# A hybrid transformer on one core: where values, projections and weighings stand in their steps, and embedded values in strips of 32 columns

## The reference

```python
att = jnp.einsum('bhtd,bhsd->bhts', q, k) * scale + jnp.einsum('bhtd,tsd->bhts', q, rk)
att = jax.nn.softmax(jnp.where(causal[None, None], att, -jnp.inf), axis=-1)
y = jnp.einsum('bhts,bhsd->bhtd', att, v) + jnp.einsum('bhts,tsd->bhtd', att, rv)
```

## Time and profile before

| | us |
|---|---|
| median of three runs | 3053.79 |
| the profiled execution | 3039.37 |
| its span, first to last instruction | 3037.6 |
| TensorE busy | 2790.9 |
| VectorE busy | 1947.6 |
| ScalarE busy | 1885.4 |
| GpSimd busy | 1055.3 |

### The profile page before, as it was taken

The page is one execution under the profiler, slowest core; times in us unless marked ns, Lnnn a source line. Parts: engine busy times, 40 slices in busy tenths (PEclk is TensorE's granted clock), DMA queues, the critical chain, the costliest instruction groups (busy, mean ns, idle before and its releaser), DMA issues.

```text
span 3037.6 us, 58842 instructions
## 1 busy us (share of the span) xinstructions
PE 2790.9 (92%) x21780; PEld 1904.2 (63%) x21780; DVE 1947.6 (64%) x5625; ACT 1885.4 (62%) x4404; POOL 1055.3 (35%) x876
## 2 busy tenths in 40 slices
PE   8889989978999999789999999898899998998997
PEld 5565647537888886378888888455355464554554
DVE  6454636376777775778888887675476324764774
ACT  6666766514666764167777777586587514875774
POOL 2222223203233230064545453354255112552551
PEclk9999999988999998999999999999999999999999
DMA  1010000000000000200000000310111001110210
GB/s 52 3 38 1 12 9 1 4 8 1 2 2 2 2 2 3 72 2 2 2 2 2 2 2 2 123 47 21 40 49 32 22 1 54 49 32 24 51 39 14
DMA packets 35262, 62.83 MB, mean 21 GB/s; under 512 B 11526, under 2 KB 15654, under 8 KB 33830
## 3 DMA queue, kind: packets, MB, share of 16 engines
q1 hardware_dynamic: 34982, 59.07, 7.0%
HBM read 23.48 MB, written 1.15 MB: 8 GB/s over the span
## 4 chain that ended last, share of the span: by engine, by line
PE 72%; DVE 10%; ACT 7%; issue 4%; POOL 3%; SPq 2%; DMA 1%; DVEq 0%; POOLq 0%; ACTq 0%
PE bank L779 62%; PE bank L1004 6%; PE bank L1119 3%; SPq L745 2%; POOL work L1903 2%; ACT bank L1245 1%; ACT work L1237 1%; ACT squared L1247 1%; DVE work L1610 1%; ACT work L1269 1%; DVE centered L1481 1%; DVE normed L1488 1%; ACT work L1361 1%; ACT squared L1241 1%; DVE work L1754 1%
## 5 line engine op out<-in xcount | busy, mean ns | idle before, releaser
L1325 ACT ACTIVATE low<-bank,low 128x512 f32<-128x512 f32 (+23 forms) x384 | 227.4, 593 | 331.0 <-DVE low L1667 326.9
L1237 ACT ACTIVATE low<-bank 128x512 f32<-128x512 f32 (+3 forms) x512 | 425.6, 941 | 0.9 <-PE bank L1004 0.9
L779 PE MATMUL bank<-table_keys,halves 128*128 128x512 f32 (+3 forms) x1536 | 419.1, 381 | 0.6 <-ACT low L1325 0.4
L779 PE MATMUL bank<-work 128*64 128x128 f32 (+6 forms) x4480 | 368.2, 291 | 41.0 <-DVE work L1557 16.1
L1667 DVE TENSOR_REDUCE low<-bank 128x1 f32<-128x512 f32 (+22 forms) x512 | 289.5, 572 | 166.1 <-PE bank L779 161.8
L779 PEld LDWEIGHTS bank<-work 128*64 128x64 f32 (+3 forms) x4480 | 266.8, 145 | 192.3 <-issue 143.5
L1857 POOL TENSOR_TENSOR halves<-squared,const 128x512 fp32r<-128x512 f32 x128 | 135.4, 1058 | 578.4 <-PE bank L779 578.4
L1237 ACT ACTIVATE work<-bank 128x512 f32<-128x512 f32 (+4 forms) x389 | 200.8, 539 | 165.1 <-PE bank L779 63.4
L779 PEld LDWEIGHTS bank<-table_keys,halves 128*128 128x128 f32 x1536 | 245.7, 192 | 55.9 <-issue 33.7
L1903 POOL TENSOR_TENSOR work<-work 128x768 f32<-128x768 f32 x128 | 187.7, 1466 | 193.6 <-DVE work L1758 190.5
L1361 ACT ACTIVATE work<-work 128x192 f32<-128x192 f32 (+1 forms) x512 | 218.8, 431 | 49.1 <-DVE work L1747 49.1
(11 more groups left out here) (198 smaller groups left out, 5900.9 us busy)
## 6 DMA issues: line engine op xcount, KB each, us to landing
work<-work SPq DMA_DIRECT2D x512, 64.0 KB, 2.0
slot<-in_wW SPq DMA_DIRECT2D x4, 1605.5 KB, 6.7
slot<-in_wA SPq DMA_DIRECT2D x4, 837.0 KB, 6.1
table_low<-embv_padded SPq DMA_DIRECT2D x2, 1536.0 KB, 6.3
table<-in_dft SPq DMA_DIRECT2D x1, 3072.0 KB, 11.8
slot<-in_wE SPq DMA_DIRECT2D x2, 584.0 KB, 3.9
const<-in_const SPq DMA_DIRECT2D x1, 1094.5 KB, 5.0
squared<-in_x SPq DMA_DIRECT2D x4, 256.0 KB, 6.1
```

Of the source, the lines that this page charges most:

```text
L779: return pe.matmul(o, l, r, start=start, stop=stop)
L1237: return act.activation(dst, src, ACT.Identity)
L1325: act.activation(PR[t.G % 4][:, 0:n], bank[t.G % 2][:, 0:n], ACT.Exp, bias=NBR[:, t.G % 4:t.G % 4 + 1], accum_out=RSR[:, t.G % 8:t.G % 8 + ...
```

## The change

Four things.

1. In A the values of window i-2 stand behind the context, the projections, the output projection and the norm, before the weighing. Since the next lane's context is now made before a lane's last values, `CN` and `QT` have two buffers.
2. In A the feed-forward is split in `a_mlp` (up and Gelu) and `a_mlp_down` (down and residual). Between the two of lane 3 stand the next layer's projection of lane 0 and its linear part, which no longer stand in step 0 (but in the first layer).
3. In W the inversion and weighing of j stand in step j, behind scores, exponentials and scaling, instead of at the head of step j+1. POOL's shift waits for the weighings ahead of it.
4. In R each embedded matmul of 64 columns is issued as two of 32.

```diff
@@ LAST_READ
-    "a_mlp": each("a_gelu", 4) + STREAM,
+    "a_mlp": each("a_gelu", 4),
+    "a_mlp_down": STREAM,
@@ make_plan, stage_a, the loop
-                if i == 0:
+                if i == 0 and layer == 0:
                     add("a_project", c=0)
                 if i < C * NT:
                     add("a_scores", c=c, w=w, i=i)
-                if i == 0:
+                if i == 0 and layer == 0:
                     add("a_linear", c=0)
                 if w == 3 and c + 1 < C:
                     add("a_linear", c=c + 1)
-                if 2 <= i <= C * NT + 1:
-                    if (i - 2) % NT == 0:
-                        held = add("a_values", c=(i - 2) // NT, w=0, i=i - 2)
-                    else:
-                        add("a_values_on", c=(i - 2) // NT, w=(i - 2) % NT, i=i - 2, tile=held)
-                    if (i - 2) % NT == NT - 1:
-                        add("a_heads", c=(i - 2) // NT, tile=held)
                 if w == 1 and c < C:
                     add("a_context", c=c)
...
                 if w == 0 and 2 <= c:
                     add("norm_scale", c=c - 2, **second)
+                if 2 <= i <= C * NT + 1:
+                    if (i - 2) % NT == 0:
+                        held = add("a_values", c=(i - 2) // NT, w=0, i=i - 2)
+                    else:
+                        add("a_values_on", c=(i - 2) // NT, w=(i - 2) % NT, i=i - 2, tile=held)
+                    if (i - 2) % NT == NT - 1:
+                        add("a_heads", c=(i - 2) // NT, tile=held)
                 if i < C * NT:
                     add("a_weigh", c=c, w=w, i=i)
@@ behind the loop
+            def mlp(c):
+                up = add("a_mlp", c=c, load=load)
+                add("a_mlp_down", c=c, load=load, tile=up)
...
                 add("norm_mean", c=0, **first)
-                add("a_mlp", c=2, load=load)
+                mlp(2)
                 add("norm_scale", c=0, **first)
                 add("norm_mean", c=1, **first)
-                add("a_mlp", c=3, load=load)
+                up = add("a_mlp", c=3, load=load)
+                add("a_project", c=0)
+                add("a_linear", c=0)
+                add("a_mlp_down", c=3, load=load, tile=up)
                 add("norm_scale", c=1, **first)
                 add("norm_mean", c=2, **first)
@@ stage_w
-                if 1 <= j <= len(pairs):
-                    lane, i, hp = pairs[j - 1]
-                    add("w_weigh", c=lane, i=i, hp=hp)
...
                 if lane_items <= r - 2 < C * lane_items:
                     scale(r - 2)
+                if j < len(pairs):
+                    lane, i, hp = pairs[j]
+                    add("w_weigh", c=lane, i=i, hp=hp)
@@ buffers
-        QT = carve(T)
+        QT = carve(2, T)
-        CN = carve(NB_A, LOC, 2, DH_A)
+        CN = carve(2, NB_A, LOC, 2, DH_A)
@@ tensor, core, embedded
-                        strip = slice(64 * (j % 2), 64 * (j % 2) + 64)
-                        last = mm(o[strip, 0:P], rows_, PT[:, t.slot, max(b, 0), :, t.cols], start=(j < 2), stop=(j + 2 >= len(blocks)))
+                        for part in range(0, QG * D_R, 32):
+                            to = 64 * (j % 2) + part
+                            last = mm(o[to:to + 32, 0:P], rows_[:, part:part + 32], PT[:, t.slot, max(b, 0), :, t.cols],
+                                      start=(j < 2), stop=(j + 2 >= len(blocks)))
@@ gpsimd, shift
                 reached(pool, "w_added", s.rotations)
+                reached(pool, "w_weighed", s.weighed)
```

More of the change, by code:

```diff
@@ L92, with __init__ @@
 class Step:
-    def __init__(self, kind, n, k, load, stream, norm, updated, shift, affine, rotations, c=0, w=0, i=0, half=0, which=0, conv=0,
+    def __init__(self, kind, n, k, load, stream, norm, updated, shift, affine, rotations, weighed, c=0, w=0, i=0, half=0, which=0, conv=0,
                  x="", pt=0, hp=0, src="", via="", dst="", gain=None, table=None, name="", u=0, tile=None):
@@ L101, in __init__ @@
         self.updated = updated
-        self.affine, self.rotations = affine, rotations
+        self.affine, self.rotations, self.weighed = affine, rotations, weighed
         self.c, self.w, self.i = c, w, i
@@ L176, in add @@
                     shift=lane_shift[lane], affine=seen.get("affine", 0),
-                    rotations=seen.get("w_add", 0), **more)
+                    rotations=seen.get("w_add", 0), weighed=seen.get("w_weigh", 0), **more)
         if kind == "norm_scale" and more["gain"]:
@@ L268, in stage_a @@
             else:
-                add("a_mlp", c=2)
-                add("a_mlp", c=3)
+                mlp(2)
+                mlp(3)
         for c in range(C):
@@ L507, in carve @@
                 return a
-            names = "abcd"[:len(shape)]
+            names = "abcde"[:len(shape)]
             return a.rearrange(f"p ({' '.join(names)}) -> p {' '.join(names)}",
@@ L675, in _ @@
                 if s.load >= 0 and s.kind not in ("weights", "tables"):
-                    stage_ends[s.load] = s.stream + (s.kind in ("fold", "a_mlp", "expert_out", "r_out", "w_mlp", "h_out"))
+                    stage_ends[s.load] = s.stream + (s.kind in ("fold", "a_mlp_down", "expert_out", "r_out", "w_mlp", "h_out"))
             def tables(s):
@@ L891, in a_mlp, with a_mlp_down @@
                     mm(take(s.k + j)[:, :], wt(s, WA, "w1", j * P, P), normed[:, s.c, :]).then_inc(tile_full, 1)
-                o = take(s.k + 4)
+            def a_mlp_down(s):
+                o = take(s.k)
                 for j in range(4):
@@ L1262, in a_context @@
             def a_context(s):
-                copy(QT[0:64, :], full(s.k)[0:64, :]).then_inc(sem("a_q_turned"), 1)
+                copy(QT[0:64, s.c % 2, :], full(s.k)[0:64, :]).then_inc(sem("a_q_turned"), 1)
             def a_scores(s):
@@ L1534, in a_context @@
                     link(dve.memset(CN[0:64], 0.0))
-                own = CN[0:64, 1:8, :, 1, :]
+                own = CN[0:64, s.c % 2, 1:8, :, 1, :]
                 link(dve.tensor_scalar(kcum[0:64, 0:7], o[:, :, 64], 1e-6, None, ALU.add))
```

18 lines of the change are left out of this document (9 added, 9 removed).

## The result

The changed kernel takes 2971.62 us (median of four, 2968.68 to 2976.36), the kernel before, run beside it, 3055.2 us (median of four, 3047.31 to 3057.44). The ratio is 0.9732, with a 95% interval of 0.9709 to 0.9755. Forecast were 2976 us within 2943 to 3022, so the time was met. Its parts were met less well, and two misses partly cancel, as will be seen. The profiled execution took 2969.49 us, span 2967.7.

A forecast was written before the change was run, and what follows sets the result against it. PE was taken as the bound, fully in R, only through its waits in A and W. Terms -22 - 37 - 14 - 5 = -78 us gave 2961 profiled; adding 14.4 gave 2976 us, range 2943 to 3022.

The forecast's parts named there:

- R, -22: R stages: embedded matmuls in strips of 32 avoid 138 strip-width changes of 0.15 us each; 22 us saved.
- Rival 2: R: 32 wide passes don't run four at a time, 111 us more; 3087 us, slower; chance 0.06.
- W, -37: W stages: weighing one step earlier removes 58.5 us of PE waits, less 21.6 of new ones; 37 us saved.
- the new waits: W: waits of PE that replace the removed ones, from DVE's loop; 5.4 us a layer, 21.6 in all.
- A, -14: A stage: values late and projection early together, with the memset; 14 us saved, bounds 0 to 29.
- values late: A: values later in a step hide PE's waits for turned weights; 0.9 of 1.3 us a lane, 10.8 in all.
- The projection early: A: next layer's projection inside the last feed-forward fills PE waits; 1.3 us three times, 3.9, despite a new wait of 3.2.
- Rival 4: A's layer start: DVE's linear part before the residual delays all norms; A gives 5 less, 2981 us; chance counted in forecast's 0.64.
- The clock, -5: Ends of layers in A and W: one in six or seven lower-clock stretches goes; 5 us saved, bounds -25 to +10.
- the 14.4 added back: Whole kernel: the runs' median lay 14.4 us above the profiled execution, so this was added to the forecast.
- (1): W and A: waits come back elsewhere, DVE held by exponentials; W gives 18, A 2; 3012 us, chance 0.23.
- (3): More than forecast: high clock stays through layers' ends and DVE's loop costs nothing; 2940 us, chance 0.07.

The follow-up runs named there:

- e1: Kernel before with only R's embedded matmuls issued in strips of 32 columns; 3026.18 us, ratio 0.9902.
- e5: Changed kernel, but in R's double steps the first tile's embedded matmuls use strips of 32 and the second tile's strips of 64; 3029.35 us, ratio 0.992.
- e9: Changed kernel, but in R the embedded matmuls stand ahead of the turn, so full-width transposes part them from values and folds; 3004.52 us, ratio 0.9848.
- e2: Kernel before with only W's inversion and weighing moved into their own step; 3022.26 us, ratio 0.9892.
- e8: Changed kernel, but W's inversion and weighing stand behind the turn of their step; 2970.03 us, ratio 0.9726.
- e3: Kernel before with only A's values late in their step and both double buffers; 3032.72 us, ratio 0.991.
- e4: Kernel before with only the next layer's projection and linear part inside A's last feed-forward; 3042.53 us, ratio 0.9969.
- e7: Changed kernel, but the linear part of the next layer's lane 0 stands behind the first scores again; 2965.06 us, ratio 0.9711.
- e6: Changed kernel, but the odd tile of R's double steps starts its blocks in the other half of the output rows; 2960.1 us, ratio 0.9701.
- e12: Changed kernel with balanced strips, linear part back behind the first scores, and norms of lanes 2 and 3 one step later; 2978.86 us, ratio 0.9766.

## Why the prediction was right, and where it was not

**R, -22.** Measured -20.9, in the changed kernel and alone (e1). The mechanism, a price for each change of strip width, is shown by e5, which adds changes and no work; 0.15 a change holds for the earlier trace rows (0.14 here), 0.13 in e5. e9 narrows it down: between narrow and full width the price is 0.14 for the way there and back, charged once for each narrow stretch. Rival 2, slower, did not come: 16 passes of 32 take the same four rounds as eight of 64 (0.47 us from 858.26 to 858.73). The Trainium skill's rule (TensorE: Matmul & The Clock Gate, Part 3, "The mechanism"), that loads overlap only where the row group differs, is not borne out: with 2304 more loads, all on the same rows, the two R stages are 20.9 us shorter.

**W, -37.** Measured: idle 24.3 less, product 25.2 less in e2. The step that was off is the new waits. I put them at 21.6, with DVE's loop as what is late next. They are 20.2 for DVE's copy, as named ("15 to 20"), but beside them 2.7 stay for POOL and ACT's copies add 6.3 (10.9 in the W stages against 4.6), which I had left out; I had also credited all 38 waits with the lost overlap of 0.16, 6.1 us, and not charged it to the new ones. With 29.2 us of new waits and without the 6.1 the forecast would have been 23, and the idle time fell by 24.3. DVE idles before its reciprocal (1.1 us) in the last lanes alone (0.3 us once a layer elsewhere), so the sign of being wrong that I had named did not come. The end of the last lane of the changed kernel, against the earlier trace rows:

```profile
2308.51 0.88 PE L787 MATMUL bank<-work 128*64 128x128 f32 x12 [2.54 <-DVE work L1766]
2309.46 1.97 PE L1131 MATMUL bank<-const,work 128*128 128x128 f32 x8
...
2312.31 1.98 PE L787 MATMUL bank<-work 128*64 128x128 f32 x16 [0.88 <-DVE work L1766]
```

One wait of 2.54 in place of 3.50 and 0.88: 2.7 had been forecast. e8 shows what really sets that loop: ACT's exponentials and its own copy, not DVE's. With DVE's copy moved out of the way the time did not change.

**A, -14.** Measured -21.4, idle 16.7. The term that was mis-sized is values late, 10.8 less 0.9: alone it gave 16.3 in idle time and 17.3 in the product (e3). I took 0.9 of 1.3 us a lane because DVE is busy without a break there. It did not take the time back: the group had the whole wait, 16.1 in 23, and 14.9 of it went. The mean of these waits is 0.70, not the 0.53 of the one row that I had taken for all. The projection early was put at 3.9 and gave about 2 (e4: 2.2 idle, 1.5 in the product). Its new wait came where it was said and is 3.84 instead of 3.2; in the changed kernel, against the earlier trace rows:

```profile
302.56 1.26 PE L787 MATMUL bank<-halves,table_keys 128*128 128x128 f32 x8
...
307.65 2.07 PE L787 MATMUL bank<-squared,const 128*128 128x512 f32 x2 [3.83 <-ACT squared L1253]
309.52 1.91 PE L787 MATMUL bank<-inner,const 128*128 128x512 f32 x2
```

Rival 4, the linear part in front of the residual, is half true: moving it back (e7) took 0.9 off the wait and 2.1 us off A's idle time.

**The clock, -5, and the 14.4 added back.** This is where two misses cancel. Between the two traces the clock loss rose, 106.6 to 109.0 us, so the -5 did not come, and the sum was -69.9 instead of -78: 8 us too hopeful. But the profiled execution before was a lucky one. It lay 15.8 below its median, and its clock loss was 106.6 where the mean is 123.1. I added that distance back to the forecast, while the profiled execution after lies only 2.1 below its own median. That put 12.3 us too much back on a sum that was 8.1 us too low, so the forecast was only some 4 us too high. That the two errors offset each other was luck. The medians differ by 83.6: about 66 by the product and about 14 by less clock loss (123.1 to 109.2); the rest is mostly that the four runs before, with their median of 3055.2, lay above the 3051.9 of the 39. The 14 were forecast as 5. Each of the four edits alone has 5 to 7.5 us less clock loss than the kernel before; for e1 to e3 that is little more than its uncertainty, for e4, with ten runs, and for the 14 of the whole change it is clear of it. Their cause stays open: shorter waits of PE go with it in e2, e3 and e4, but e1 takes no wait away. My count of the lower clock was short, too: in the A and W stages of the profiled execution before it holds for 104 us (twice the clock loss there, 18.8 + 22.2 + 11.1), not 85.

The rivals: the waits came back only in part (1); slower (2) was wrong; no high clock through the layers' ends (3); (4) as above.

## What to carry to other kernels

Strips of one width should stand together on TensorE: in this kernel each further stretch of narrow passes cost 0.13 to 0.15 us, more than a round of passes (0.11), and an uneven load of the strips cost whole rounds (e6). Where two engines copy halves of the same tile, the wait names only the later; taking it away gained nothing here, where the other half came as late (e8). A wait of PE that was filled moved to the next thing that its slow producer owed (e12), so it is the producer's chain that should be shortened or started earlier. And a single profile is to be set against the median with its granted clock at hand: span times clock told apart effects of a few us that the medians hid, though not where the clock itself differed much (e9).

## What was not expected of the hardware

Identical code ran at different clocks from run to run. R0 of e3, with the code of the kernel before:

```profile
689.20:1163.10 473.90, 473.20 (x5395) 401.20 (x5395) 344.72 (x1097) 301.42 (x761) 138.00 (x136) 0.96 0.01 2
```

473.9 us instead of 464.8, with no wait more. In it the lower clock, granted in the E stage ahead, holds for 44.4 us on end, from 680.5, and in the kernel before for 23.9 from 691.0. In each of the three waits of 3.8 in A, or just behind it, the granted clock falls to 0.50, 1.2 GHz, for 3.4, 6.8 and 6.8 us; in the changed kernel, beside the wait that ends at 307.65:

```profile
305.70:312.50 6.80, 4.85 (x10) 2.78 (x11) 3.49 (x14) 3.46 (x12) 2.06 (x2) 0.50 0.35 127
```

This wait costs itself and then, by an estimate, some 2.4 us more, half of the 4.85 us for which PE is busy in this stretch: passes of 512 columns take 0.93 instead of 0.43 us each there. In e12 this second price, 18.7 us more clock loss in A, was more than twice the first, 8.3.
